# Rows loaded ahead of weights, block tables made in two halves, and products with unread results at four places before the first expert block

## The reference

```python
x = x + tanh(g_xattn[1]) * attend(layernorm(x), ctx)        # 2nd attention: scores, softmax, weighted context
# 2nd feed-forward part, on xt = layernorm(x), 2048 tokens:
logits = xt @ Wr + br
pr, idx = top_k(logits, 2); w = softmax(pr)                  # two of eight experts for each token
for e in range(8):
    h = silu(xt @ W1[e] + b1[e]) * (xt @ W2[e] + b2[e])      # 128 -> 512
    y = y + (h @ W3[e] + b3[e]) * cw[:, e:e+1]               # 512 -> 128, weighted
x = x + tanh(g_ffn[1]) * y
```

## Time and profile before

| | before |
|---|---|
| median of three runs | 630.33 us |
| the profiled execution's own time | 636.85 us |
| its span, first to last instruction | 635.0 us |
| mean granted TensorE clock | 0.941 |
| TensorE busy | 561.3 us (88%) |
| VectorE, ScalarE, GpSimd busy | 65%, 51%, 32% |
| chain that ended last: PE, DMA, DVE, SPq, POOL, issue | 64%, 9%, 8%, 7%, 4%, 4% |

### The profile page before, as it was taken

One profiled execution on the slowest core, in us unless ns is written; L12 is line 12 of the kernel. 1 busy time (PEld: TensorE's weight loads), 2 busy tenths in 40 slices (PEclk: granted clock), 3 DMA queues, 4 the chain that ended last, 5 costly groups with the idle time before them and its releaser, 6 DMA issues.

```text
span 635.0 us, 9965 instructions
## 1 busy us (share of the span) xinstructions
PE 561.3 (88%) x3295; PEld 331.8 (52%) x3307; DVE 412.8 (65%) x1054; ACT 320.8 (51%) x652; POOL 206.4 (32%) x217
## 2 busy tenths in 40 slices
PE   2776899999998799999999999999786969899991
PEld 1432344444453244444444445545575969899991
DVE  4759968989347599678334566557786656344455
ACT  2535646666656875555454527282544424344440
POOL 4907701010032363001782310001654655233330
PEclk9786969999998999999999999999978889899996
DMA  7376791000039500000012002000005878899965
GB/s 268 101 191 101 181 197 26 3 3 3 2 120 325 191 0 1 1 0 0 0 57 76 0 1 20 0 1 0 29 25 149 291 224 270 280 292 328 311 212 206
DMA packets 48010, 71.19 MB, mean 112 GB/s; under 512 B 11110, under 2 KB 35112, under 8 KB 47672
## 3 DMA queue, kind: packets, MB, share of 16 engines
q1 hardware_dynamic: 44968, 65.61, 35.3%
q0 software_dynamic: 2272, 4.69, 2.0%
q10 hardware_dynamic: 720, 0.27, 0.2%
HBM read 59.18 MB, written 21.29 MB: 127 GB/s over the span
## 4 chain that ended last, share of the span: by engine, by line
PE 64%; DMA 9%; DVE 8%; SPq 7%; POOL 4%; issue 4%; ACT 3%; POOLq 0%; DVEq 0%
PE psum L1953 21%; PE psum L2224 7%; PE psum L1898 5%; PE psum L1755 4%; PE psum L1768 4%; PE psum L2235 4%; POOL sorted_x L792 3%; PE psum L1900 3%; SPq L513 3%; PE psum L1950 2%; PE psum L1776 2%; DMA wb<-in_wall_dram 2%; PE psum L1732 2%; DMA xb<-sorted_x 2%; PE psum L1782 2%
## 5 line engine op out<-in xcount | busy, mean ns | idle before, releaser
L1953 PE MATMUL psum<-hidden,ew 128*128 128x512 f32 x320 | 143.8, 592 | 0.6
L880 ACT ACTIVATE probs<-psum 128x512 f32<-128x512 f32 x128 | 74.6, 598 | 50.0 <-PE psum L1755 49.6
L1953 PEld LDWEIGHTS psum<-hidden,ew 128*128 128x128 f32 x320 | 60.7, 190 | 69.4 <-issue 68.1
L1164 DVE TENSOR_REDUCE negmax<-psum 128x4 f32<-128x1024 f32 x64 | 76.9, 1210 | 19.9 <-PE psum L1732 19.5
L2224 PE MATMUL psum<-xbT,wb 128*128 128x128 f32 x624 | 81.2, 286 | 1.3 <-DMA wb<-in_wall_dram 1.3
L2224 PEld LDWEIGHTS psum<-xbT,wb 128*128 128x128 f32 x624 | 77.5, 202 | 1.8 <-DMA wb<-in_wall_dram 1.7
L1081 ACT ACTIVATE silu_g<-psum,wb 128x128 f32<-128x128 f32 x156 | 44.6, 368 | 66.0 <-PE psum L2224 66.0
L1647 DVE SCALAR_TENSOR_TENSOR gated<-psum,wb,silu_g 128x128 f32<-128x128 f32 x156 | 43.9, 344 | 48.2 <-ACT silu_g L1081 41.6
L817 POOL DMA_INDIRECT sorted_y<-yb,xb x39 | 37.5, 962 | 69.0 <-DVE yb L1639 66.9
L1755 PE MATMUL psum<-stacks 50*128 50x256 bf16 x256 | 51.0, 291 | 5.0 <-DMA stacks<-maxT 2.9
L2235 PE MATMUL psum<-wb,gated 128*128 128x128 f32 x312 | 42.8, 281 | 3.4 <-DVE yb L1639 3.4
(11 more groups left out here) (254 smaller groups left out, 954.6 us busy)
## 6 DMA issues: line engine op xcount, KB each, us to landing
wb<-in_wall_dram SPq DMA_DIRECT2D x39, 516.0 KB, 5.1
wb<-in_wall_dram SPq DMA_DIRECT2D x39, 256.0 KB, 5.0
sorted_x<-in_slots_dram SPq DMA_DIRECT2D x1, 9815.0 KB, 32.6
stacks<-stacked SPq DMA_DIRECT2D x12, 384.0 KB, 8.4
xb<-sorted_x SPq DMA_DIRECT2D x39, 65.0 KB, 3.6
stacked<-parts SPq DMA_DIRECT2D x6, 384.0 KB, 3.4
back<-sorted_y SPq DMA_DIRECT2D x4, 512.0 KB, 5.5
stacked<-parts SPq DMA_DIRECT2D x6, 256.0 KB, 3.3
```

The lines of the kernel that those rows point to most:

```text
L880: nc.scalar.activation(probs[:, g % 2, h % 4, :, :], s2[n % 2].rearrange("p (k q) -> p k q", k=2), ACT.Exp, scale=float(HD) ** -0.5).then_ ...
L1164: nc.vector.tensor_reduce(negmax[:, p].rearrange("p h q -> p (h q)"), psum[:, i:i + 2, :].rearrange("p h (q k) -> p (h q) k", q=2), AX.X, ...
L1953: last = nc.tensor.matmul(dst, ew2[:, j, cols], hidden[:, c, k - 1, j, :], start=False, stop=(j == 3))
```

## The change

- **Rows ahead of weights.** In `load_blocks` (blocks 9 and 17) the weights of the first block are no longer loaded ahead of the wait for the rows; three row loads come first, not four after it.
- **Tables in halves.** The early table is written after `fuse(5)`, `maxima2(7)` and `third_stats(2)`, not before them. The middle table's `blocks_of` stays in block 4, its writing moves to block 5. The late table's `blocks_of` moves from block 8 to block 7.
- **Rows sent in other groups.** GpSimd sends five rows of chunk 0 ahead of `rstd_of_chunk(3, 1)`, not six; three of chunk 2 ahead of the first scatter, not two; and two of chunk 3 in each of the blocks 3 to 6, not one in each of the blocks 3 to 10.
- **Products with unread results.** `keep_busy(dst, n)` issues n products (bf16, 128x128 stationary, 256 columns) into a bank that nobody reads before it is written again: 6, 12, 10 and 8 of them at four places.

```diff
--- before.py
+++ after.py
@@ -631,11 +631,10 @@
 
             def load_blocks(first, end, table, rows):
                 sp.wait_ge(table, 1)
-                load_weights(first)
                 sp.wait_ge(rows, 16 * GR)
-                for j in range(first, first + AHEAD + 1):
+                for j in range(first, first + AHEAD):
                     load_rows(j)
-                for j in range(first + 1, end):
+                for j in range(first, end):
                     load_weights(j)
                     if j + AHEAD < end:
                         load_rows(j + AHEAD)
@@ -798,9 +797,9 @@
                 nc.gpsimd.tensor_tensor(w_top[:, tc, 1], euler[:, 0:TC], gap2[:, tc], ALU.pow).then_inc(w2nd_ready, 1)
 
             second_weights(0)
-            send_rows(0, range(0, 6))
+            send_rows(0, range(0, 5))
             rstd_of_chunk(3, 1)
-            send_rows(0, range(6, GR))
+            send_rows(0, range(5, GR))
             rstd_of_chunk(2, 2)
             pool.wait_ge(w2nd_ready, 2)
             send_rows(1, range(0, 1))
@@ -809,7 +808,7 @@
             rstd_of_chunk(3, 2)
             rstd_of_chunk(3, 3)
             second_weights(2)
-            send_rows(2, range(0, 2))
+            send_rows(2, range(0, 3))
 
             for j in range(BLOCKS):
                 pool.wait_ge(yb_ready, j + 1)
@@ -817,11 +816,11 @@
                 nc.gpsimd.indirect_dma_start(sorted_y, bass.IndirectOffsetOnAxis(ap=home, axis=0), yb[:, j % X_BUFS, :],
                                              None).then_inc(yb_out[j % X_BUFS], 16)
                 if j < 3:
-                    send_rows(2, range(2 * j + 2, 2 * j + 4))
+                    send_rows(2, range(2 * j + 3, min(2 * j + 5, GR)))
                 if j == 1:
                     second_weights(L)
-                if 3 <= j < 3 + GR:
-                    send_rows(L, range(j - 3, j - 2))
+                if 3 <= j < 7:
+                    send_rows(L, range(2 * j - 6, 2 * j - 4))
 
         @block.scalar
         def _(act):
@@ -1608,10 +1607,10 @@
             blocks_of(0)
             fuse(4)
             maxima2(6)
-            table_of_blocks(0, early_table, EARLY, early_ready)
             fuse(5)
             maxima2(7)
             third_stats(2)
+            table_of_blocks(0, early_table, EARLY, early_ready)
             layer_norm_rows(2)
             sums_of(3)
             fuse(6)
@@ -1658,9 +1657,11 @@
                     slots_of(L)
                 if j == 4:
                     blocks_of(1)
+                if j == 5:
                     table_of_blocks(1, middle_table, MIDDLE, middle_ready)
+                if j == 7:
+                    blocks_of(2)
                 if j == 8:
-                    blocks_of(2)
                     table_of_blocks(2, late_table, LATE, late_ready)
                 if j == 10:
                     expert_shares()
@@ -2172,9 +2173,17 @@
                     last = nc.tensor.matmul(bank[7][:, at:at + E], ones, seen[:, c + 1, :], start=True, stop=True)
                 last.then_inc(rank_psum, 1)
 
+            def keep_busy(dst, n):
+
+                for _ in range(n):
+                    nc.tensor.matmul(dst[:, 0:2 * P], identb[:], route_b[:], start=True, stop=True)
+
             second_scores(2)
             second_scores(3)
             route_ranks(0)
+            pe.wait_ge(soft_done, 6 * NC)
+            pe.wait_ge(probsT_ready, 2)
+            keep_busy(bank[2], 6)
             transpose_probs(2)
             transpose_probs(3)
             weigh_context(2)
@@ -2182,6 +2191,8 @@
             refine_up(2)
             refine_up(3)
             refine_down(2)
+            pe.wait_ge(x3_ready, 4)
+            keep_busy(bank[5], 12)
             rows_to_columns(1)
             route_logits(1)
             refine_down(3)
@@ -2197,6 +2208,8 @@
             weigh_context(5)
             second_scores(7)
             transpose_probs(6)
+            pe.wait_ge(x3_ready, 5)
+            keep_busy(bank[4], 10)
             transpose_probs(7)
             weigh_context(6)
             rows_to_columns(2)
@@ -2206,6 +2219,7 @@
             pe.wait_ge(x2_ready, NC)
             pe.wait_ge(x3_ready, B)
             pe.wait_ge(probsT_ready, B)
+            keep_busy(bank[1], 8)
 
             def rows_T(j):
                 pe.wait_ge(xb_in[j % X_BUFS], 16 * (j // X_BUFS + 1))
```

## The result

The change made the kernel faster, by about half of the forecast: ratio 0.9918 (0.989 to 0.9947) to the kernel before on the same chips, 20 runs of each. That is 5.2 us (0.0082 x 630.33), with an interval of 3.3 to 6.9; 9.9 us (1.57%) were forecast. The median of the change's runs is 626.75 us, 0.15 above the upper end of the forecast range (617.0 to 626.6); the ratio on 630.33 gives 625.2, inside it and 4.8 above the forecast of 620.4.

What follows compares the result with a forecast made beforehand. TensorE was taken to bound the kernel, with DMA a close second and gains only in earlier gaps; 2.7 + 0.3 + 4.3 + 0.4 + 3.7 - 1.5 = 9.9 us off 630.33 gave 620.4 us, range 617.0 to 626.6.

Steps and rivals of the forecast that it cites:

- A: Up to block 1: earlier sends, filled waits and the later early table bring everything SyncE issues 2.7 us sooner.
- F: Blocks after the reordered loads: weights are issued with less slack ahead of their `up`, a loss of 1.5 us (0 to 3).
- I take it that the clock then stays up: After the filled gap ahead of `rows_to_columns(1)`: full clock, so chunk 1's logits lose about 0.8 us.
- What follows them is bound by VectorE, so the slower products behind them are worth nothing more: Behind chunk 1's logits: VectorE sets the pace, so a full clock for TensorE's products gains nothing further.
- B: `up(1)` at full clock would give 1.5 us; mostly taken back by GpSimd's sends, so 0.3 (0 to 1.5).
- C: Blocks 5 to 9: halved middle table and rows issued ahead of weights start `up(9)` sooner, 4.3 us (2.4 to 4.9).
- Now they start with 4.2 to 5 us: Slack of weights ahead of their `up` after the reordering, where the steady stretch had 5.8 us.
- D: The late table in halves, with one short TensorE idle behind it at block 9: 0.4 us gained.
- E: Block 17: rows issued ahead of weights remove the 2.98 us wait and half clock of `up(16)`; 3.7 us (2.0 to 4.3).
- the steady stretch turns DMA bound: Rival: 30 blocks from 9 on lose over 0.38 us each, making the kernel slower, 634 us; chance 0.06.
- The clock falls all the same: Rival: half clock remains behind the gaps at the first blocks, 9 and 17; gain 6.6 us, 623.7 us; chance 0.25.
- One wait for another: Rival: weights of blocks 9 and 17, issued later, land late; gain 3.7 us, 626.6 us; chance 0.14.

Runs made afterwards that it cites:

- full_p4: The unedited change, profiled on one chip beside two executions of the kernel before; stretch 182.2 us, theirs 188.1 and 185.2.
- full_again: The unedited change run once more on another chip, against the kernel before; ratio 0.9899, stretch 181.6 us.
- loads_only: Kernel before with rows ahead of weights at blocks 9 and 17 and chunks 2 and 3 sent in larger groups; ratio 0.9943, stretch 179.8 us.
- products_only: Kernel before with only the four groups of unread products added; ratio 1.0021.
- before_p4: The kernel before, unedited, one of two profiled executions beside the change on one chip; their stretches were 188.1 and 185.2 us.
- tables_old: The change with all three tables back at their old places; ratio 0.9922 to the kernel before, stretch 179.5 us.
- tables_old_p4: The edit of tables_old, profiled beside the change and the kernel before on one chip; stretch 180.7 us, the change's 182.2.
- early_table_old: The change with only the early table back at its old place; ratio 0.9853 to the kernel before, stretch 181.4 us.

## Why the prediction was right in its places and wrong in its size

The sign and the places were right; the size was 9.9 us and is 5.2. The miss of 4.7 is made of three parts: 2.2 us since the sum was made against one execution whose stretch (190.0) was 2.2 above the mean of three (187.8); 2.0 us in the terms (against that execution the change's mean gains 7.9, not 9.9); and 0.5 that the timing does not resolve. That the terms are off by only 2.0 is partly luck, as the first part flatters them. Against the means they miss by 4.2: A by 1.9 and F by 2.3, and the others are right to within 0.5.

**A, forecast 2.7, came as 0.8.** The early steps came as described: `rstd` starts 1.0 us sooner, `xp` is ready 13.8 us from the mark, not 14.8, in every execution with five sends ahead, and with the twelve products the logits run at full clock in all three executions of the change. The last send of chunk 1 lands after 2.3 us, not 5.0. The steps that failed are "I take it that the clock then stays up" and "What follows them is bound by VectorE, so the slower products behind them are worth nothing more". Behind the wait ahead of the next probabilities the clock comes down, at 26 to 29 us from the mark in the change and in full_p4, and there it holds up `transpose_probs`, `fuse(5)` and so the table, which now stands behind `fuse(5)`. Weights of block 0 go out at 36.9 from the mark. In full_again the fall came at 22 to 25 us, and they go out at 35.4, where I had put them (480.5 - 444.98 = 35.5); that run has the 2.35 us of gain at `up(1)`. The first rows go out 2.7 us sooner there, as forecast, and 1.2 sooner in the other two. Then the rows of block 0, issued right behind the weights, took 3.6 us to reach TensorE (480.46 to 484.11), not 1.8. By the Trainium skill ("DMA: Bandwidth & Descriptors", Queues, rings and completion order) descriptors are consumed in ring order, and this row agrees. I saw it and gave it no price, since idle time stood behind block 0; but behind the wait `up(0)` runs at half clock, 3.0 to 3.5 us in the three executions.

With the early table at its old place the stage is 45.2 on average (44.9, 45.3, 45.5), 1.1 less than the change's. Set side by side by where the clock fell, the move costs nothing where it fell early (45.1 against 44.9 and 45.3) and 1.5 us where it fell late (46.8 and 47.1 against 45.5). In those three executions `up(0)` and `up(1)` both run at full clock, 2.01 and 2.03 us. They differ from loads_only (47.4, `up(0)` 3.37 us) ahead of block 1 by the products and by chunk 0's five sends, so these two together are worth some 2 us beside an early table at its old place. Which of them it is was not tested apart: products_only has the products with six sends, and 47.3 in its one profiled execution.

**B, forecast 0.3, came as about 0.2** up to `up(5)` (14.1 us behind `up(1)` on average, not 14.3). `up(1)` takes 2.0 to 2.4 us, not 3.48, but in before_p4 it takes 2.03 as well. The blocks behind it start hardly sooner.

**C, forecast 4.3, came as 4.8 at block 9, and F took much of it back.** The stall at `down(5)` went as forecast, and `up(7)` is 2.4 us sooner. `up(9)` starts 28.9 us behind `up(1)` on average (28.9, 29.0, 28.7), where the kernel before has 33.8 (34.4, 34.3, 32.8): 4.9 us sooner, B's 0.2 among them. That is C's mechanism, and nearly its upper bound. Its weights land in 3.7 to 3.9 us, as I had them (4.2). The step that failed is F: "Now they start with 4.2 to 5 us", a loss of 1.5 us for all that follows. That takes the first load's landing time for that of the next two. From issue to `up` it is 5.3 to 5.8 us at block 10 and 6.3 to 7.6 at block 11, in the three executions, and from `up(9)` to `up(12)` it is 11.8 us on average (11.3, 12.6, 11.6), where the kernel before has 9.0 in each. That is 2.8 us lost at once, and 1.0 more behind block 18: 3.8, not 1.5, and beyond F's bound of 3.

The table's lateness of 1.3 us was as I had worked it out (1.4); but I priced it for the rows and the weights of block 9 alone, while SyncE issues everything behind it. And I booked the stall at `down(5)`, 1.92 us, as a gain of its own. It lay in parallel with the loads that end the next waits: with the whole table TensorE loses 1.9 us there, the loads run meanwhile, and behind them stand waits for weights of only 0.7 to 1.3 us in all, not 3.4 to 3.9. From `up(1)` to `up(12)` it is 38.6 us with the table whole (38.0, 38.3, 39.6 in loads_only, tables_old, tables_old_p4), 40.7 with it halved. Of these 2.1 us the later issue explains 1.0 to 1.3 in the first two; in tables_old_p4 the issue is no sooner, and it gains only 0.7 on the change beside it. Why the loads of the change then also take longer to land is not shown.

**D, forecast 0.4,** can't be told apart: it lies within the scatter of the third stage.

**E, forecast 3.7, came as 3.8.** The mechanism is as described, with one wait for another: the weights of block 17 did not make TensorE wait at all in the three executions, where I had about 1 us, and the rows did for up to 0.78 us. On the chips that compare, all runs with these loads show 17.1 to 18.2 us here, all without them 21.0 to 21.6.

**F behind block 18** came as -1.0, over three executions of each, though one of before (77.6) is as long as all of the change. TensorE's waits for weights there are 1.75, 0.44 and 1.16 us in the change, 1.34 (the two late landings of the forecast), 0 and 0 before. The DMA share rose from 0.90 to 0.94 and the rate from 294 to 314 GB/s; a block takes 2.89 us in the change and 2.80 to 2.88 before. The rival that the steady stretch turns DMA bound needed 0.38 us a block more, and is refuted.

**The rivals.** "The clock falls all the same" put the gain at 6.6 us, "One wait for another" at 3.7; the 5.2 lie midway. The first named the clock at the first blocks. The second named late weights and took F at 3, nearest to what F was, and was too low on C and on E. The two are not exclusive, and what happened is a half of each. 0.25 and 0.14 were too little beside 0.5 for a sum in which every term had to come true.

What stays open: the traces say that the change without its table moves would gain about 2 us more (180.1 against 182.1, two executions and three), and the timings, at half a per cent, neither show nor exclude it (0.9922 and 0.9918; on the same chip 0.9922 and 0.9899). For loads_only, whose trace says the same, the timing speaks against it. early_table_old has the lowest ratio, 0.9853, without being told apart from the change either.

## What to carry to other kernels

- A stall that lies beside a running load is not a gain of its own. Ask for each stall that is to go what else was under way in it; here 1.9 us of TensorE's wait ran beside the issue and the landing of the next blocks' loads.
- When a queue's order is turned round, price everything that stands behind the displaced load, block by block with the landing times of a busy queue (here 4.0, 5.5 and 6.3 us to `up`, not 4.2 each), and expect the slack to be missing right there. The first load behind the turn can be on time and the next two late.
- Make the sum against several executions by stages between fixed marks. A single one held 2.2 of the 9.9 us as its own bad luck, and a filled gap may only be followed by a fall of the clock at the next gap. A full clock behind a filled gap proves nothing until it is missing without the filling; here two executions had it with no products at all.

## What the runs showed of the hardware

- The same program, upstream of any edit, has its mark at 440.7, 443.1, 445.0, 450.9 and 452.6 us in five executions of the kernel before. The stretch behind the mark spans 185.2 to 190.0 on the chips that compare.
- The granted clock falls at other gaps from one execution of a program to the next. Windows of full_again, where the first profiled execution of the change had 1.00 in both places: at 463 to 467 us 0.57, and at block 10 0.66, with the DMA engines at a share of 1.02 and 369 GB/s.

```profile
463.00:467.00 4.00, 3.37 (x11) 2.08 (x9) 3.42 (x14) 1.88 (x8) 3.42 (x4) 0.57 0.05 17
520.00:525.00 5.00, 4.32 (x24) 4.32 (x25) 1.07 (x4) 1.41 (x5) 0.72 (x1) 0.66 1.02 369
```

- In the kernel before, it is `up(1)` that runs at half clock in two executions (3.48 and 3.59 us, `up(0)` 1.96 and 2.01) and `up(0)` in the third (3.47, `up(1)` 2.03).
- A short transfer issued behind a large one lands late: 65 KB of rows took 3.6 to 3.7 us from issue to TensorE behind 772 KB of weights in the three executions of the change, and 1.8 to land in a quiet queue.
- The first piece of a block's weights, 516 KB, took 3.7 to 3.9 us to land when it was the first of a row of loads (block 9 of the change), and from issue to `up` it was then 5.3 to 5.8 at the next block and 6.3 to 7.6 at the one behind it.
